# An attention and butterfly kernel on one core: coefficient loads, early copies and the way of the tokens changed

## What is computed

```python
def _L0_xattn_ref(q, k, v):
    kv = jnp.swapaxes(k * v, 0, 1)
    def step(r, kv_t):
        r = DECAY * r + kv_t
        return (r, r)
    ...
    return q * jnp.swapaxes(rs, 0, 1)
def _L0_ffn_ref(x, W_exp, b_exp, up_weights, up_bias, down_weights, W_con, b_con, down_bias):
    h = jnp.einsum('bsd,dh->bsh', x, W_exp) + b_exp
    h = butterfly(h, up_weights, D_HIDDEN)
    h = jax.nn.gelu(h + up_bias, approximate=False)
    h = butterfly(h, down_weights, D_HIDDEN)
    y = jnp.einsum('bsh,hd->bsd', h, W_con) + b_con
    return y + down_bias
x = x + _L0_xattn_ref(_layernorm(x, axis=-1), ctx_1024, ctx_1024)
x = x + _L0_ffn_ref(_layernorm(x, axis=-1), ...)
```

## Time and profile before

| | us |
|---|---|
| median of 3 runs | 2779.0 (2778.31 to 2779.04) |
| profiled execution | 2779.58 |
| its span, first to last instruction | 2777.8 |
| PE busy | 2739.9 (99%) |
| DVE busy | 2129.9 (77%) |
| ACT busy | 1127.5 (41%) |
| POOL busy | 401.5 (14%) |
| mean granted PE clock | 0.993 of full |

### The profile page before, as it was taken

How to read it: one execution, slowest core, us unless ns; L and a number is a source line. 1 busy time by engine, 2 the same in 40 slices (tenths; PEclk the granted TensorE clock), 3 DMA queues, 4 the chain that set the end, 5 groups by cost and what they waited for, 6 DMA issues and landing times.

```text
span 2777.8 us, 35037 instructions
## 1 busy us (share of the span) xinstructions
PE 2739.9 (99%) x12159; PEld 2259.3 (81%) x12159; DVE 2129.9 (77%) x3562; ACT 1127.5 (41%) x1707; POOL 401.5 (14%) x577
## 2 busy tenths in 40 slices
PE   8889999999999999999999999999999999999999
PEld 6668888888888888888888888888888888888887
DVE  8968787787878778787877878777787877788533
ACT  5653434334343443434343343433434343343432
POOL 4821011110101101010110201011020111101000
PEclk8999999999999999999999999999999999999999
DMA  9795675758567575856758475675847657585543
GB/s 272 261 294 176 195 201 174 217 154 252 158 199 205 167 225 154 236 171 191 212 164 233 153 223 183 179 221 160 241 151 222 186 173 225 159 243 152 183 151 99
DMA packets 294837, 542.57 MB, mean 195 GB/s; under 512 B 37430, under 2 KB 101078, under 8 KB 277766
## 3 DMA queue, kind: packets, MB, share of 16 engines
q1 hardware_dynamic: 287760, 536.82, 64.8%
q0 software_dynamic: 1488, 2.27, 0.4%
q10 hardware_dynamic: 5414, 1.25, 0.3%
HBM read 445.83 MB, written 60.82 MB: 182 GB/s over the span
## 4 chain that ended last, share of the span: by engine, by line
PE 94%; DVE 1%; POOL 0%; DMA 0%; ACT 0%; issue 0%; ACTq 0%; DVEq 0%; POOLq 0%
PE ps L1739 44%; PE ps L1760 25%; PE ps L1773 25%; DMA raw<-kv 0%; PE ps L1634 0%; PE ps L1840 0%; DVE w1r L1195 0%; DVE xop L1195 0%; DVE x L1252 0%; POOL raw L512 0%; DVE raw L1249 0%; DVE st L1255 0%; POOL x L760 0%; ACT xop L904 0%; PE ps L1639 0%
## 5 line engine op out<-in xcount | busy, mean ns | idle before, releaser
L1739 PE MATMUL ps<-xop,w1r 128*128 128x512 f32 x5376 | 1364.1, 389 | 2.5 <-DVE xop L1283 1.6
L1739 PEld LDWEIGHTS ps<-xop,w1r 128*128 128x128 f32 x5376 | 1008.9, 188 | 213.0 <-DVE xop L1283 2.3
L1760 PE MATMUL ps<-w2r,ghi 128*128 128x512 f32 x2048 | 630.5, 389 | 0.0
L1773 PE MATMUL ps<-w2r,ghi 128*128 128x512 f32 x2032 | 625.8, 389 | 0.0
L995 ACT ACTIVATE st<-ps 128x512 f32<-128x512 f32 x384 | 229.7, 598 | 839.8 <-PE ps L1739 839.8
L1389 DVE TENSOR_TENSOR x<-ps,x 128x512 f32<-128x512 f32 x508 | 348.9, 687 | 280.9 <-PE ps L1773 278.5
L1760 PEld LDWEIGHTS ps<-w2r,ghi 128*128 128x128 f32 x2048 | 384.4, 188 | 79.8
L1773 PEld LDWEIGHTS ps<-w2r,ghi 128*128 128x128 f32 x2032 | 381.2, 188 | 79.8 <-DVE glo L1412 0.4
L1407 DVE TENSOR_TENSOR g<-ps,st 128x512 f32<-128x512 f32 x384 | 262.8, 684 | 212.1 <-PE ps L1739 212.1
L999 ACT ACTIVATE g<-g,gelu_bias 128x512 f32<-128x512 f32 x384 | 275.4, 717 | 362.6 <-DVE g L1407 361.7
L1412 DVE TENSOR_TENSOR glo<-g,ghi 128x512 fp32r<-128x512 f32 x510 | 347.6, 702 | 79.2 <-ACT ghi L1013 79.2
(11 more groups left out here) (171 smaller groups left out, 1620.0 us busy)
## 6 DMA issues: line engine op xcount, KB each, us to landing
w1r<-w_products SPq DMA_DIRECT2D x889, 256.0 KB, 3.3
w2r<-w_split SPq DMA_DIRECT2D x126, 1024.0 KB, 4.9
x<-in_x_dram SPq DMA_DIRECT2D x128, 256.0 KB, 7.3
raw<-kv SPq DMA_DIRECT2D x496, 64.0 KB, 2.1
out_dram<-x SPq DMA_DIRECT2D x120, 256.0 KB, 4.1
kv<-in_ctx_dram SPq DMA_DIRECT2D x64, 256.0 KB, 7.4
raw<-in_ctx_dram SPq DMA_DIRECT2D x64, 256.0 KB, 5.4
wexp<-in_L_ffn_W_exp_dram SPq DMA_DIRECT2D x4, 1024.0 KB, 11.0
```

The lines of the kernel that those rows point to most:

```text
L1739: last = nc.tensor.matmul(bank[:, :], w1r[:, slot, w, c * P:(c + 1) * P], xop[:, XPOS[m], v, c, :], start=(opens and i == 0), stop=(i == l ...
L1760: last = nc.tensor.matmul(ps_ya[j][:, :], g[:, p % 2, q, j * P:(j + 1) * P], w2r[:, p % 2, kk, w, :], start=(p == 0 and kk == 0 and i == 0 ...
L1773: last = nc.tensor.matmul(ps_yb[:, :], g[:, p % 2, q, j * P:(j + 1) * P], w2r[:, p % 2, kk, w, :], start=(kk == 0 and i == 0), stop=(kk == ...
```

## The change

1. SP loads the coefficients of the two `PARTED` stages before the expansion weights; ACT keeps the others (`load_lanes`, `load_stages`).
2. On ACT `coefs_hi(0, ...)` and the four casts of the choosing matrices (from DVE) come first, then `WT` copies with the rest between them; `square(0, 0)` comes after eight `low_up` and the last four `WT`. On DVE the two `WT` copies and the casts are gone and memsets come later.
3. PE makes the spreads of the low stages before and between twelve turnings, eight `low_up`, the last four turnings, then the other `low_up`. `low_up` is kept in `Z`, and `low_folded` is gone.
4. For the first super-tile `normalise` writes to `kv`, and eight new fold steps `tokens` turn it with PE transposes, copied by ACT straight into `raw`; the DVE transposes and the moves of that super-tile are gone. `high_matrix(1)` on POOL waits for `xn_ready`.
5. Token loads and output stores in all super-tiles are cut by row `j` over all 128 partitions, no longer by group `g` over 32; each of the last rows is stored by SP and by ACT in one transfer of two groups instead of two transfers.

```diff
-        FOLD = [("WT", k, "dve" if k in (1, 3) else "act") for k in range(KH)]
-        FOLD += [("low_up", k, "act") for k in range(KH)]
+        FOLD = [("WT", k, "act") for k in range(12)]
+        FOLD += [("low_up", k, "act") for k in range(KH // 2)]
+        FOLD += [("WT", k, "act") for k in range(12, KH)]
+        FOLD += [("low_up", k, "act") for k in range(KH // 2, KH)]
...
-        FOLD += [("high_dn", r, "act") for r in range(R)]
+        FOLD += [("high_dn", r, "act") for r in range(R - 3)]
+        FOLD += [("tokens", i, "act") for i in range(2)]
+        FOLD += [("high_dn", r, "act") for r in range(R - 3, R)]
+        FOLD += [("tokens", i, "act") for i in range(2, J)]
...
-        FOLD += [("back", k, "act") for k in range(KH)]
+        FOLD += [("back", k, "act") for k in range(10)]
+        FOLD += [("tokens", i, "act") for i in range(J, J + 2)]
+        FOLD += [("back", k, "act") for k in range(10, KH)]
+        FOLD += [("tokens", i, "act") for i in range(J + 2, 2 * J)]
...
-                return low_folded[:, i, :], whole
+                return Z[:, i, :], whole
...
+            if kind == "tokens":
+                return raw[:, i // J, :, :].rearrange("p c (g j i) -> p c g j i", g=G, j=J)[:, :, :, i % J, :],\
+                    whole.rearrange("p (c g i) -> p c g i", c=KD, g=G)
...
-        def load_coefs(eng, weights, dn):
+        def load_lanes(eng, weights, dn):
...
-            for stage in range(len(WHOLE), LOWS):
+
+        def load_stages(eng, weights, dn, stages):
+            for stage in stages:
...
-            for g in groups:
-                eng.dma_start(out_rows[g, end * 2 + 1][:, j, :], xs[end % 2][Q * g:Q * g + Q, J + j, :])\
-                  .then_inc(out_stored, NX)
+            eng.dma_start(out_rows[groups, end * 2 + 1, :, j, :],
+                          xs[end % 2][Q * groups.start:Q * groups.stop, J + j, :]).then_inc(out_stored, NX)
...
             def load_tokens(dst, h, rows, t, loaded):
-                for g in range(G):
-                    sp.dma_start(dst[Q * g:Q * g + Q, J * h:J * h + J, :], rows[g, t]).then_inc(loaded, NX)
+                for j in range(J):
+                    sp.dma_start(dst[:, J * h + j, :], rows[:, t, :, j, :]).then_inc(loaded, NX)
...
+            load_stages(sp, up_w, 0, reversed(PARTED))
...
-                sp.dma_start(up_dram[k], low_folded[:, k, :]).then_inc(up_stored, NX)
+                sp.dma_start(up_dram[k], Z[:, k, :]).then_inc(up_stored, NX)
...
-            sp.wait_ge(xn_turned, J)
-            move_xT(sp, 0, 0, xT_moved[0])
-            move_xT(sp, 0, 1, xT_moved[0])
...
-            sp.wait_ge(xn_turned, 2 * J)
-            move_xT(sp, 1, 0, xT_moved[1])
-            move_xT(sp, 1, 1, xT_moved[1])
...
-                    for g in range(G):
-                        sp.dma_start(out_rows[g, u * 2 + h], xs[par][Q * g:Q * g + Q, J * h:J * h + J, :])\
-                          .then_inc(out_stored, NX)
+                    for j in range(J):
+                        sp.dma_start(out_rows[:, u * 2 + h, :, j, :], xs[par][:, J * h + j, :]).then_inc(out_stored, NX)
...
+                            sp.wait_ge(fold_made, fold_at("tokens", 2 * J - 1) + 1)
...
-                store_last_row(sp, j, (0, 1))
-            sp.wait_ge(out_stored, end * (2 * G * NX) + J * G * NX)
-            sp.wait_ge(last_stored, G * NX)
+                store_last_row(sp, j, slice(0, G // 2))
+            sp.wait_ge(out_stored, end * (2 * J * NX) + 2 * J * NX)
+            sp.wait_ge(last_stored, J * NX)
...
+            nc.gpsimd.memset(parts_zero(1), 0.0).then_inc(parts_zeroed[1], 1)
...
-            pool.wait_ge(sel_zero, 2)
+            pool.wait_ge(sel_zero, 1)
...
-            load_coefs(pool, down_w, 1)
-            nc.gpsimd.memset(parts_zero(1), 0.0).then_inc(parts_zeroed[1], 1)
+            load_lanes(pool, down_w, 1)
+            load_stages(pool, down_w, 1, range(len(WHOLE), LOWS))
...
-            pool.wait_ge(xn_turned, J)
+            pool.wait_ge(xn_ready, J)
...
-            first_moves(0)
...
-            first_moves(1)
...
-            for g in range(G):
-                pool.dma_start(out_rows[g, end * 2], xs[end % 2][Q * g:Q * g + Q, 0:J, :]).then_inc(last_stored, NX)
+            for j in range(J):
+                pool.dma_start(out_rows[:, end * 2, :, j, :], xs[end % 2][:, j, :]).then_inc(last_stored, NX)
...
-            load_coefs(act, up_w, 0)
+            load_lanes(act, up_w, 0)
+            load_stages(act, up_w, 0, PLAIN)
...
-                    act.wait_ge(xT_moved[0], moved_by(u))
+                    if first:
+                        wait_kept(act, "tokens", J - 1)
+                    else:
+                        act.wait_ge(xT_moved[0], moved_by(u))
...
-            for k in range(KH):
-                if k == KH // 2:
-                    for stage in PARTED:
-                        coefs_hi(0, stage)
-                    top_hi(0)
-                    act.dma_start(bias_row[:, :], b_con.partition_broadcast(P)).then_inc(bias_loaded, NX)
-                    act.dma_start(bias_tmp, down_bias.partition_broadcast(P)).then_inc(bias_loaded, NX)
-                    for stage in PARTED:
-                        coefs_hi(1, stage)
+            for stage in PARTED:
+                coefs_hi(0, stage)
+            act.wait_ge(sel_padded, 2)
+            act.wait_ge(sel_ready, 2 * len(PARTED))
+            for lane in (0, Q):
+                act.activation(sel_parts[lane:lane + Q], part_choice[0:Q], ACT.Copy).then_inc(sel_rounded, 1)
+            act.dma_start(bias_row[:, :], b_con.partition_broadcast(P)).then_inc(bias_loaded, NX)
+            act.dma_start(bias_tmp, down_bias.partition_broadcast(P)).then_inc(bias_loaded, NX)
+            fold_step("WT", 0)
+            top_hi(0)
+            fold_step("WT", 1)
+            act.wait_ge(top_sel_ready, 2)
+            for lane in (0, Q):
+                act.activation(top_sel[lane:lane + Q], top_choice[0:Q], ACT.Copy).then_inc(top_sel_ready, 1)
+            for k in range(2, 10):
...
-            for k in range(KH):
+            for stage in PARTED:
+                coefs_hi(1, stage)
+            for k in range(10, 12):
+                fold_step("WT", k)
+            for k in range(KH // 2):
                 fold_step("low_up", k)
-                if k == 1:
-                    square(0, 0)
+            for k in range(12, KH):
+                fold_step("WT", k)
+            square(0, 0)
+            for k in range(KH // 2, KH):
+                fold_step("low_up", k)
...
-            for r in range(12, R):
+            fold_step("high_dn", 12)
+            for i in range(2):
+                fold_step("tokens", i)
+            for r in range(13, R):
...
+            for i in range(2, J):
+                fold_step("tokens", i)
...
+            for i in range(J, J + 2):
+                fold_step("tokens", i)
...
+            for i in range(J + 2, 2 * J):
+                fold_step("tokens", i)
...
-                store_last_row(act, j, (2, 3))
+                store_last_row(act, j, slice(G // 2, G))
...
+            nc.vector.memset(parts_zero(0), 0.0).then_inc(parts_zeroed[0], 1)
...
+                if u == 0:
+                    xn = kv[:, j, :]
+                    if j == 0:
+                        dve.wait_ge(x1_ready, t * J + J)
+                    if h:
+                        dve.wait_ge(fold_made, fold_at("tokens", j) + 1)
+                elif j:
+                    dve.wait_ge(xn_turned, turned_by(t, j))
...
+                if u == 0:
+                    return
...
-            for k in range(KH // 4):
-                fold_step("WT", k)
-
-            dve.wait_ge(sel_padded, 2)
-            dve.wait_ge(sel_ready, 2 * len(PARTED))
-            nc.vector.tensor_copy(sel_parts[0:Q], part_choice[0:Q]).then_inc(sel_rounded, 1)
...
-            dve.wait_ge(top_sel_ready, 2)
-            for lane in (0, Q):
-                nc.vector.tensor_copy(top_sel[lane:lane + Q], top_choice[0:Q]).then_inc(top_sel_ready, 1)
...
+                if kind == "tokens":
+                    pe.wait_ge(xn_ready, i + 1)
...
+                    elif kind == "tokens":
+                        last = nc.tensor.transpose(o, kv[:, i % J, block_c], ident[:, :])
...
+            spread_low(WHOLE)
+            for k in range(12):
+                if k % 4 == 0:
+                    pe.wait_ge(wexp_loaded[k // 4], NX)
+                if k == 2:
+                    spread_low(PLAIN)
+                if k == 4:
+                    spread_low(PARTED)
+                if k == 6:
+                    spread_top((0, 1))
+                if k == 8:
+                    spread_top((2,))
+                if k == 10:
+                    spread_top((3,))
+                fold_step("WT", k)
+            pe.wait_ge(low_matrix_ready, 1)
...
-                    spread_low(range(LOWS))
...
-            spread_top((3,))
-            pe.wait_ge(low_matrix_ready, 1)
```

(35 more changed lines are left out.)

72 lines of the change are left out of this document (26 added, 46 removed).

## The result

| | us, median | runs | ratio to before, 95% interval |
|---|---|---|---|
| before | 2779.0 | 2778.3 to 2779.0 | |
| after | 3273.7 | 3272.0 to 3280.7 | 1.1789 [1.1773, 1.1804] |

The kernel is slower by 494.6 us. A fourth run of the kernel before took 3442.9 us and is left out, as a run in a slower state of the chip. The profiled execution's span is 3270.4 us, 492.6 more than before.

What follows compares the result with a forecast made beforehand. TensorE, busy 99% of the span, was taken to bound the kernel. Steady stretch with clock 336, start-up 13, tail 14 and edits -3 made +360 on 2779.6: 3140 us, 8 in 10 from 2800 to 3300.

Steps and rivals of the forecast that it cites:

- Few engines, the same ones: Token loads and output stores cut by rows run on four fixed DMA engines, not sixteen: 3140 us, chance 0.74.
- Price of a packet: Time of a 2 KB packet on one of four busy engines: 84 ns taken, bounds 67 and 113 ns.
- Arrival of x: Walk through the four engines' backlog per super-tile: first half of x at 383 us, where VectorE takes it at 359.29.
- inside the 24: Per super-tile, product loads queued behind x land 18 us late, within the 24 us that TensorE loses anyway.
- Clock: After TensorE's idle time in each super-tile its clock has fallen: 3 us, from 1.4 us for four matmuls.
- Start-up: To 168 us: first loads on four engines delay TensorE by 14 us (0 to 25), 13 in the final sum; edits -3.
- The edits of the start-up: Turning of the first tokens and new beginning together, before 168 us: -3 us, from -7 to +6.
- The turning: First tokens turned by TensorE, so the token sum starts 2.7 us earlier, against ScalarE's copies: -1 us (-2.7 to +2.1).
- The beginning: Coefficients first, casts on ScalarE, later squares, four transposes fewer at 69 us: -2 us (-4 to +4).
- Tail: After the last matmul, last rows stored on two engines: +15 us (0 to +18), 14 in the final sum.
- few engines, but room in the queue: Rival: engines vary between transfers or the queue has room; only start-up and tail pay: 2806 us, chance 0.11.
- spread over all: Rival: rows are cut over all engines as before, only the start-up edits count: 2776 us, chance 0.15.

Runs made afterwards that it cites:

- e6_rows_each_group: e3_loads with each of the four groups loaded by a transfer of its own, outermost count 32 instead of 4: 2781.1 us.
- e3_loads: The kernel before with only the loads of context and x cut by rows, stores still cut by group: 3034.6 us.
- e4_stores: The kernel before with only the output stores of the body and GpSimd's last four cut by rows: 2935.1 us.
- e11_x_by_rows: The kernel before with only the loads of x of super-tiles 1 to 15 cut by rows: 2906.5 us.
- e7_x_by_pool: e3_loads with the loads of x of super-tiles 1 to 15 issued by GpSimd through its own queue, same descriptions: 3017.9 us.
- e2_rows: The kernel before with all token loads, output stores and last rows cut by rows, no other part of the change: 3273.4 us.
- e1_groups: The kernel after with token loads, output stores and last rows cut by group again, all else kept: 2776.6 us.
- e10_tokens_alone: e1_groups with the beginning as in the kernel before, leaving only the tokens turned by TensorE and low_up kept in Z: 2771.1 us.
- e8_tail: e1_groups with only the stores of the last four rows cut as in the kernel after: 2792.6 us.

## Why the prediction was right, and where its sizes were off

Direction, mechanism and range held (2800 to 3300; measured 3273.7). Of +494.6 it had +360. By its own steps:

**Few engines, the same ones.** Right, and now shown: share 0.24 to 0.28 in after, 0.13 with outer count 2, and the loss gone in e6_rows_each_group with an outer count of 32. One part of the evidence was none: that GpSimd's transfers into wcon have a time to landing says nothing of their engines, as its last stores in after have one too. The rule of the Trainium skill that the prediction set against the change ("DMA: Bandwidth & Descriptors", section "Why a DMA increments its semaphore by 16 and not by 1") agrees: four engines for count 4, two for count 2. Of its second half, the lowest-numbered ones, the rows show only that they are always the same.

**Price of a packet.** 84 ns taken; 78 to 82 measured from 100 to 105 GB/s.

**Arrival of x.** The walk had VectorE start at 383 by 84 ns, 43 us after the first store; measured 45.0 (616.61 - 571.62). But the walk let the loads queue up behind the stores, while in fact SP doesn't issue them until the stores have landed. The two give nearly the same arrival, as the four engines have the same work either way: the number came out for a reason that the walk hadn't considered. They don't give the same to those behind SP: this is the step that failed first. The prediction had the product loads 18 us late "inside the 24". In fact SP was held up in the stores, so products wanted at 595.7 came at 604.1, ahead of x's lateness and not inside it (8.39 us), and again behind x (3.94), while the wait for x itself fell to 10.51. The three make 22.8 us. Over the whole stretch TensorE stands for 343 us where 14 x 21 = 294 was forecast, +49 in the sum. Of the 343, 17 lie in the first and the last super-tile (loads without stores, stores without loads), which the forecast left out; the other fourteen have 23.3 each.

**Clock.** The term that was mis-sized most. I took 3 us per super-tile, from four matmuls after one stand. There are three stands, and the granted clock was 0.51 to 0.72 in the 5 us windows in which TensorE took up work again. Measured: 110 us, or 7.9 for each of 14 super-tiles, against 42 forecast: +68 us, half of what was missing. The cost shows in every run that starves TensorE, by its busy time in part 1 of their pages against 2739.9. For e3_loads:

```profile
PE 2809.6 (93%) x12159; PEld 2294.7 (76%) x12159; DVE 2127.6 (70%) x3562; ACT 1128.0 (37%) x1707; POOL 400.0 (13%) x577
```

| run | TensorE stood after the start-up, us | stands of 1 us and more | busy longer by, us | for each stand | for each us |
|---|---|---|---|---|---|
| after | 343 | 46 | 110.8 | 2.4 | 0.32 |
| e3_loads | 162 | 32 | 69.7 | 2.2 | 0.43 |
| e4_stores | 105 | 25 | 43.8 | 1.8 | 0.42 |
| e11_x_by_rows | 84 | 21 | 44.1 | 2.1 | 0.53 |
| e7_x_by_pool | 174 | 17 | 43.8 | 2.6 | 0.25 |

The price goes by the number of stands, 1.8 to 2.6 us each, rather than by their length, by which it is 0.25 to 0.53 for each microsecond. So the 3 us were not far off for one stand; that there would be three was missed. (The lower bound of +180 left the clock out: 13 x 14 is 182, and 224 with 3 us more in each super-tile.)

**Start-up.** The forecast had +13 for few engines and -3 for the edits; e2_rows has the first alone: its last wait is at 193.00, +24.4, and the edits take 7.7 of it back in after (185.27). The first `high_up` came at 68.90 ("near 70"), but there was a second stall, which the prediction didn't have: ScalarE's second squares wait for the other half of the context, which SP issues behind the reload of Z. The prediction had named such a wait as the sign that the order of the loads was mis-sized.

```profile
68.90 5.26 PE L1666 MATMUL ps<-HX,Z 128*128 128x128 f32 x32 [8.27 <-ACT HX L944]
...
95.90 3.62 PE L1666 MATMUL ps<-HX,Z 128*128 128x128 f32 x16 [13.18 <-ACT W1f L863]
```

```profile
93.26 1.91 ACT L867 ACTIVATE raw<-raw 128x2048 f32<-128x2048 f32 x1 [14.41 <-DMA raw<-in_ctx_dram]
```

The 7.7 us don't show in the medians of e2_rows and after (3273.4, 3273.7). At 423 us, where the second wait for x ends, after is still 7.1 us ahead of e2_rows (423.68, 430.77); it falls back in the 13 waits after that. Why is not settled; single runs of either lie 6 to 9 us apart.

**The edits of the start-up.** Their sum was right (-3; e1_groups is 1.8 below before, its start-up 2.7), its terms were not. The turning was forecast at -1 (-2.7 to +2.1) and gave about -7: I let VectorE's last weight split end at 138.5 as before and so had the token sum 2.7 us earlier. But four of the eight removed VectorE transposes, 2.8 us, stand shortly ahead of that split (117.7 to 125.6 us) and weren't taken off it; in e10_tokens_alone it starts 2.3 us earlier (131.46 for 133.73). And its two rows, 2.58 and 2.28 us before (the second in the earlier trace rows), take 1.02 and 1.23. Before, GpSimd adds two rows of bias beside them, and it is such an addition that goes with a slow VectorE instruction: the same token split takes 2.29 us beside one and 1.21 beside GpSimd's issues, with the moves under way.

```profile
126.73 3.66 POOL L760 TENSOR_TENSOR x<-x,bias_row 128x512 f32<-128x512 f32 x2
...
134.73 2.69 POOL L760 TENSOR_TENSOR x<-x,bias_row 128x512 f32<-128x512 f32 x2
```

```profile
129.18 2.29 DVE L1283 TENSOR_TENSOR xop<-raw,xop 128x1024 fp32r<-128x1024 f32 x1
...
132.00 1.21 DVE L1283 TENSOR_TENSOR xop<-raw,xop 128x1024 fp32r<-128x1024 f32 x1
```

In e10_tokens_alone the additions are over at 129.85, before the split begins. The beginning was forecast at -2 (-4 to +4) and cost about 5: the squares came 5 us later, as feared, but the four transposes that were to pay for it lie behind the place where it hurts.

**Tail.** +15 forecast (0 to 18); 16.0 in e8_tail, 22.7 in after. There GpSimd's four stores are cut by rows too, and the DMA share is still 0.40 from 3245 to 3250; In e4_stores, where of the tail they alone are cut by rows, it ends 12.5 us after TensorE's last matmul instead of 6.8, and 5.7 more on the 16.0 is near the 22.7. That the last rows wait behind them is argued, not shown.

The rivals: "few engines, but room in the queue" (2806) and "spread over all" (2776) both fell with e2_rows.

## What to carry to other kernels

When a transfer is cut another way, read the outermost count of both its sides before anything else: here the same bytes, packets and rows cost 256 us or 3 us by whether that count was 4 or 32 (the latter in four times as many transfers). A transfer on few engines is late itself, makes the queue's issuer stand, and holds up everything that the issuer would do next, so its price is read from who is behind it in the issuer's order. And each stall of TensorE is to be charged with its clock: count the stalls, and add about 2 us (1.8 to 2.6 here, for mean lengths of 4 to 10 us) for each.

## What was not expected of the hardware

- The issuing engine is held up by a crowded queue: eight stores of 256 KB took SP 8.13 us to issue on sixteen engines and 20.78 on four, eight loads 3.65 and 12.48.
- With the same descriptions eight loads through GpSimd's queue used more than ten engines' time where SP's queue has four, and were hardly faster with it: 17 of 256 us came back (e7_x_by_pool).
- Two engines move 50 GB/s and four 100, the others idle: 25 GB/s for one.
- VectorE's split of 128x1024 took 2.29 us beside a GpSimd addition and 1.21 without one.
